# Attention and graph layers over 128 small graphs: the loop over the steps written out, and the instructions that carried its waits left out

## The chip, the cores and the metric

The kernel runs on one core of one Trainium2 chip. The metric is the device time of one execution in microseconds (us). TensorE (PE) has two clock levels, 1.2 and 2.4 GHz; a granted clock of 1.00 in the profile is the upper one.

## The reference

The input x holds 128 batches of 128 rows by 256 columns in float32, adj is one 128 by 128 matrix. Two layers are added to x one after the other:

```
h = relu(layernorm(x));            # over the 256 columns
A = adj @ h[b];  C = adj @ h[b] + bias
x = x + max over the columns of relu(A[:, None, :] + (C - A)[:, :, None])   # C - A = bias, so relu(max A + bias)
h = relu(layernorm(x))
q, k, v = split(h @ w_qkv);  8 heads of 32
a = softmax(where(adj == 0, -inf, q k^T / sqrt(32)));  o = (a v) @ w_proj + b_proj
x = x + o + layernorm(o) * gamma + beta
```

The first layer adds one number per row, so the second layernorm sees the same h as the first, and the kernel computes h once.

## The kernel before, in words

**Tiling.** A step handles four batches (G = 4), so there are 32 groups of work. Matrix products run in fp16 with a value split in a high and a low part, three products in place of one. The products with p_sb and v_sb, the softmax sums and the transposes are fp32.

**Stages.** A group passes through four consecutive steps t: products with adj and the projections to q, k, v (flag `a`), scores and their row maxima (`sc`, one step later), scores transposed, exponentials and their product with v (`e`, two later), normalising, projecting and storing (`d`, three later). So 32 groups take 35 steps, t = 0 to 34. In the middle every step has all stages at once, each of a different group.

**Order.** Each engine has its own instruction stream. In each, a list named `ORDER` names the pieces of a step, and `step(t, ...)` walks it. TensorE's list is
```
ORDER = ("K0 S0 S1 R0 S2 Q0 S3 R1 Q1 N0 E0 R2 O0 E1 E2 E3 L0 O1 R3 K1 S4 S5 O2 S6 S7 L1 O3 N1 M0 E4 E5 E6 "
         "P0 P1 Q2 P2 P3 Q3 P4 P5 E7 V0 P6 P7 V1").split()
```
K and N lay the mask into the four score banks of PSUM (`put_mask`, L339 to L346), S are scores (L368), M0 transposes the row maxima (L377), E transposed scores (L396), P the product with v and the sums (L416, L419), Q and V projections (L319, L332), L the first layer (L304), R and O the end of a group (L431, L443, L446). Engines wait for one another by counting semaphores: the k-th use waits for a value that grows with t.

**The loop.** `pipeline(eng, step)` runs steps 0 to 3 written out, then a loop in the hardware's sequencer (`eng.Fori`) over t = 4, 7, ..., 25 with three steps in its body (so 24 steps, 8 passes and 7 returns to its top), then steps 28 to 34 written out. Inside the loop the value of a wait is computed from the loop's register.

**Carriers.** Some instructions do no work of the kernel. In `put_mask` the first matmul (L339) writes one column that the next ones overwrite; it is there so that it takes the wait with a register's value. `act_cell` on ScalarE (L531), `dve_cell` on VectorE (L651, L713) and `carry_waits` on GpSimd (L822) are the same. They are in the written-out steps as well.

**Other places that are named below.** Row maxima: VectorE reduces each score bank (`row_max`, L674); M0 waits for all eight of them. The maxima then go through ScalarE (`max_high`, crow, L566) and VectorE (`max_low`, crow, L680), and P0 waits for that. The two fp16 parts of q and k go from `pairs` to `stack` by DMAs that SyncE (SP) issues: `stack_heads`, L273, twelve for each half of the heads, Q0 and Q1 of its list `C0 Q0 M0 Q1`; the scores S4 to S7 of the next step need those of Q1. ScalarE issues one transposing DMA a step (L532), ahead of its part of Q2. POOL is GpSimd.

Of the kernel before, what the change touches and what calls it, by code (L numbers as in the profile page):

```python
# [31 lines left out]
STEPS = B // G  # L32
P = 128
# [23 lines left out]
def build(nc, x, adj, bias0, w_qkv, w_proj, b_proj, gamma, beta, out):  # L57
# [3 lines left out]
    with ExitStack() as ctx:  # L61
# [38 lines left out]
        wp_hi = sb("wp_hi", [P, DC, D], F16)  # L100
        wp_lo = sb("wp_lo", [P, DC, D], F16)
        mhalf = sb("mhalf", [P, G])
        dve_cell = sb("dve_cell", [P, 2])
        pool_cell = sb("pool_cell", [P, 8])
        act_cell = sb("act_cell", [P, 1])

        x_sb = sb("x_sb", [P, SLOTS, G, D])
        y_sb = sb("y_sb", [P, G, D])
# [103 lines left out]

        def wait(eng, s, value):

            if not isinstance(value, int) or value > 0:
                eng.wait_ge(s, value)

        def pipeline(eng, step):


            def at(t):
                step(t, t % SLOTS, t < STEPS, 1 <= t <= STEPS, 2 <= t <= STEPS + 1, t >= 3, t + 1 < STEPS, t + 2 < STEPS,
                     t + 3 < STEPS)

            for t in range(SLOTS + 1):
                at(t)
            with eng.Fori(SLOTS + 1, STEPS - 2 * SLOTS, SLOTS) as t:
                for k in range(SLOTS):
                    step(t + k, (k + 1) % SLOTS, True, True, True, True, True, True, True)
            for t in range(STEPS - SLOTS - 1, STEPS + SLOTS):  # L230
                at(t)

        block = ctx.enter_context(nc.Block())

# [1 line left out]
        @block.sync  # L236
        def _(sp):
            nc.sync.dma_start(x_sb[:, 0], xg[0]).then_inc(x_loaded, 16)
            nc.sync.dma_start(adj_sb[:], adj).then_inc(core_load, 16)
            nc.sync.dma_start(w_sb[:], w_qkv.rearrange("(c p) n -> p c n", p=P)).then_inc(core_load, 16)  # L240
            nc.sync.dma_start(wp_sb[:], w_proj.rearrange("(c p) n -> p c n", p=P)).then_inc(c_load, 16)
            nc.sync.dma_start(bias0_sb[:], bias0.rearrange("(p o) -> p o", o=1)).then_inc(c_load, 16)
            for vec, dst in ((gamma, gamma_sb), (beta, beta_sb), (b_proj, bproj_sb)):
                nc.sync.dma_start(dst[:], vec.rearrange("(o d) -> o d", o=1).to_broadcast([P, D])).then_inc(c_load, 16)

            def copy_x(t):

                wait(sp, copied, 16 * t)
                nc.sync.dma_start(out.rearrange("(g b) n d -> g (b n) d", b=G)[t],
                                  x.rearrange("(g b) n d -> g (b n) d", b=G)[t]).then_inc(copied, 16)  # L250

            def max_rows(g, slot):

                for part, done in enumerate((chi_ready, clo_ready)):
                    sp.wait_ge(done, g + 1)
                    row = stack[STACK + part:STACK + part + 1, slot, 0].rearrange("p h b n -> p (h b) n")
                    nc.sync.dma_start(row, crow[:, part]).then_inc(crow_in, 16)

            def stack_heads(t, slot, j):
                if j == 0:  # L260

                    wait(sp, st_psum, UNITS * (t - 2))
                both = sp.snap(4 * t + 2 * j + 2) if not isinstance(t, int) else 4 * t + 2 * j + 2
                wait(sp, qkhi_ready, both)
                wait(sp, qklo_ready, both)
                for i in range(HC):
                    head = slice(HD * i, HD * (i + 1))

                    high = bass.AP(pairs[:].tensor, HD * i * PAIRS + 2 * j * G * N,
                                   [[PAIRS, HD], [(2 * DC + 1) * G * N, 2], [1, G * N]])  # L270
                    for blk, src in enumerate((high, pairs[head, 0, j], pairs[head, 1, j])):
                        dst = stack[blk * HD:(blk + 1) * HD, slot, :, HC * j + i]
                        nc.sync.dma_start(dst.rearrange("p s b n -> p s (b n)"), src).then_inc(stacked[j], 16)  # L273

            ORDER = ("C0 Q0 M0 Q1").split()

            def step(t, k, a, sc, e, d, prep, norm, load):
                for what in ORDER:
                    kind, i = what[0], int(what[1])
                    if kind == "C" and a:  # L280
                        copy_x(t)
                    elif kind == "Q" and a:
                        stack_heads(t, k, i)
                    elif kind == "M" and sc:
                        max_rows(t - 1, (k + 2) % SLOTS)

            pipeline(sp, step)


        @block.tensor  # L290
        def _(pe):
# [43 lines left out]
                mm.then_inc(v_psum, 1)  # L335

            def put_mask(mask):

                nc.tensor.matmul(sc_ps[0][:, 0, 0:1], identb[:], mask[:, 0, 0:1], start=True, stop=False,  # L339
                                 skip_group_check=True)  # L340
                for c in range(ROW_TILES):
                    for r in range(ROW_TILES):
                        rows = slice(HD * r, HD * (r + 1))
                        nc.tensor.matmul(sc_ps[r][HD * c:HD * (c + 1)], identb[rows, HD * r:HD * (r + 1)],  # L344
                                         mask[rows, c].unsqueeze(1).to_broadcast([HD, HC, N]), start=True, stop=False,
                                         skip_group_check=True)  # L346

            def mask_scores(g, j, e):

                if j == 0:  # L350
                    wait(pe, p_ready, UNITS * (g - 1))
                    if isinstance(g, int):
                        wait(pe, smax_ready, UNITS * g)
                elif e:
                    pe.wait_ge(p_ready, UNITS * (g - 1) + SC_SLOTS)
                else:
                    pe.wait_ge(smax_ready, UNITS * g + SC_SLOTS)
                put_mask(mask_q)
# [94 lines left out]
            O_BEFORE_M = sum(what[0] == "O" for what in ORDER[:ORDER.index("M0")])  # L453

            def step(t, k, a, sc, e, d, prep, norm, load):
                if isinstance(t, int) and t == 1:

                    pe.wait_ge(pool_const, 7)
                    pe.wait_ge(act_const, ACT_CONST)
# [30 lines left out]
                    elif kind == "O" and d:  # L490
                        project_o(t - 3, i, sc)

            pipeline(pe, step)


        @block.scalar
        def _(act):
            act.wait_ge(pool_zero, 4)
            act.wait_ge(adjT_ps, 1)
            nc.scalar.activation(adjT_hi[:], sc_ps[0][:, 0, :], ACT.Copy, scale=WS).then_inc(act_const, 1)  # L500
            act.wait_ge(core_load, 16 * 2)
# [24 lines left out]
            def transpose_h(t, par):  # L526
# [1 line left out]
                wait(act, v_psum, 2 * (t - 2))  # L528
                act.wait_ge(hhi_ready, G * (t + 1))
                act.wait_ge(hlo_ready, G * (t + 1))  # L530
                nc.scalar.activation(act_cell[:], pool_cell[:, 0:1], ACT.Copy)  # L531
                nc.scalar.dma_start_transpose(hT[:, par].rearrange("p a b c n -> p (a b c) n"),  # L532
                                              h_parts[:, par].rearrange("p a b d -> p (a b d)")).then_inc(hT_in, 16)

# [60 lines left out]
                     "E7 A2 V0 A3 V1 L0").split()  # L595

            def step(t, k, a, sc, e, d, prep, norm, load):
                if isinstance(t, int) and t == 1:
                    take_masks()
                for what in ORDER:  # L600
                    kind, i = what[0], int(what[1])
# [30 lines left out]
            load_x(2, 2)  # L632
            later_constants()
            transpose_h(0, 0)
            pipeline(act, step)


        @block.vector
        def _(dve):
# [8 lines left out]
            def aggregate_x(t):  # L648
                dve.wait_ge(stats1, G * (t + 1))
                wait(dve, norm1, 4 * t)  # L650
                nc.vector.memset(dve_cell[:, 0:1], 0.0)  # L651
                for b in range(G):
                    nc.vector.bn_aggr(mv1[:, b], st1[:, b]).then_inc(mv1_ready, 1)

# [54 lines left out]
            def aggregate_o(g):  # L709
                dve.wait_ge(stats2, G * (g + 1))  # L710
                wait(dve, norm2, 4 * g)
                wait(dve, tw_ready, G * g)
                nc.vector.memset(dve_cell[:, 1:2], 0.0)  # L713
                for b in range(G):
                    nc.vector.bn_aggr(mv2[:, b], st2[:, b]).then_inc(mv2_ready, 1)

# [88 lines left out]
            stats_x(1, 1)  # L805
            aggregate_x(1)
            later_constants()
            pipeline(dve, step)


        @block.gpsimd
        def _(pool):
# [4 lines left out]
                nc.gpsimd.affine_select(out=m[:], in_=m[:], compare_op=ALU.not_equal, fill=1.0, base=0,  # L817
                                        pattern=[[-1, P]], channel_multiplier=1).then_inc(pool_const, 1)

            def carry_waits(cell):  # L820

                nc.gpsimd.tensor_tensor(pool_cell[:, cell:cell + 1], pool_cell[:, 0:1], pool_cell[:, 0:1], ALU.add)  # L822

            def invert_std_x(t, par):

                pool.wait_ge(mv1_ready, G * (t + 1))
                wait(pool, h_ready, G * (t - 2))
                carry_waits(1)
                nc.gpsimd.tensor_scalar(ve1[:], mv1[:, :, 1], 1.0, EPS, ALU.mult, ALU.add).then_inc(norm1, 1)
                nc.gpsimd.tensor_scalar(negm1[:], mv1[:, :, 0], -1.0, 0.0, ALU.mult, ALU.add).then_inc(norm1, 1)  # L830
                pool.wait_ge(norm1, 4 * t + 1)
# [17 lines left out]
            def normalise_o(g):  # L849

                pool.wait_ge(mv2_ready, G * (g + 1))
                wait(pool, y_ready, G * g)
                carry_waits(3)
                nc.gpsimd.tensor_scalar(ve2[:], mv2[:, :, 1], 1.0, EPS, ALU.mult, ALU.add).then_inc(norm2, 1)
                nc.gpsimd.tensor_scalar(base2[:], mv2[:, :, 0], 1.0, 0.0, ALU.mult, ALU.add).then_inc(norm2, 1)
                pool.wait_ge(norm2, 4 * g + 1)
# [5 lines left out]
            def keep_l0(g, par):  # L862
                pool.wait_ge(l0_ready, g + 1)
                wait(pool, norm2, 4 * g)
                carry_waits(4)
                nc.gpsimd.tensor_scalar(l0_kept[:], l0[:, par], 1.0, 0.0, ALU.mult, ALU.add).then_inc(kept, 1)

            def widen(g, b):
                if b == 0:
                    pool.wait_ge(norm2, 4 * (g + 1))  # L870
                    carry_waits(2)
                nc.gpsimd.tensor_scalar(w2_sb[:, b], gamma_sb[:], rstd2[:, b:b + 1], 1.0,
                                        ALU.mult, ALU.add).then_inc(w2_ready, 1)

# [27 lines left out]
            def later_constants():  # L902
# [1 line left out]
                nc.gpsimd.memset(sel_sum[:], 0.0).then_inc(pool_zero, 1)  # L904
                nc.gpsimd.memset(sel_row[:], 0.0).then_inc(pool_zero, 1)
                nc.gpsimd.memset(lo_pick[:], 0.0).then_inc(pool_zero, 1)
                pool.wait_ge(pool_zero, 7)
                v = sel_sum[:].rearrange("p u (r e) -> p u r e", e=UNITS)
                nc.gpsimd.affine_select(out=v, in_=v, compare_op=ALU.not_equal, fill=SUM_SEL, base=0,
                                        pattern=[[1, UNITS], [0, HD // UNITS], [-1, UNITS]],  # L910
# [11 lines left out]
                    nc.gpsimd.memset(stack[STACK:ROWS, par, 1], MS).then_inc(ms_rows, 1)  # L922
                    pool.wait_ge(ms_rows, par + 1)

            nc.gpsimd.memset(pool_cell[:], 0.0).then_inc(pool_zero, 1)
            pool.wait_ge(pool_zero, 4)
            pool.wait_ge(dve_const, 1)
            invert_std_x(0, 0)
            for b in range(G):
# [1 line left out]
            later_constants()  # L931
            invert_std_x(1, 1)
            pool.wait_ge(c_load, 16 * 5)
            pipeline(pool, step)
            pool.wait_ge(stored, 16 * STEPS)


# [18 lines left out]
```

## Time and profile before

| | us |
|---|---|
| median of 3 runs | 870.18 (869.18 to 874.16) |
| the profiled execution | 871.38 |
| its span, from the first to the last instruction | 869.70 |
| PE busy | 765.6 (88%) |
| VectorE, ScalarE, GpSimd busy | 613.9, 500.7, 424.7 |
| mean granted clock | 0.957 |
| instructions in the trace | 31246, of them 22482 on PE (matmuls and weight loads) |

PE is the busiest engine. Its busy share is near full in all slices of the span but the first few and the last three. An idle time in a row stands in brackets with what ended it; "issue" there means that the engine waited for nothing that the profile shows. Matmuls of PE overlap, so the distance between two starts tells what one costs, not its own duration.

### The profile page before, as it was taken

What the parts mean: (1) busy time and instruction counts of PE and PEld (TensorE: products, weight loads), DVE (VectorE), ACT (ScalarE), POOL (GpSimd) and SP (SyncE); (2) the same over time, 40 slices, a digit from 0 to 9 for tenths busy, and PEclk for the clock granted to TensorE, in tenths of its full rate; (3) what the DMA queues carried; (4) which work ended last, traced back from release to release, by engine and by line L of the source; (5) the groups of instructions that cost most, each with busy time, mean ns of one, the idle gap of its engine ahead of it and who ended that gap; (6) DMA issues with size and microseconds to landing.
All of it is one profiled execution on the core that took longest, in us unless ns stands there. A gap on an engine that the chain in (4) does not pass through costs nothing.

```text
span 869.7 us, 31246 instructions
## 1 busy us (share of the span) xinstructions
PE 765.6 (88%) x11241; PEld 518.0 (60%) x11241; DVE 613.9 (71%) x1552; ACT 500.7 (58%) x1192; POOL 424.7 (49%) x853
## 2 busy tenths in 40 slices
PE   0668999989998998999899899899989999999662
PEld 0234666656665665666566566666666666666441
DVE  3744777767876775777688678677777777877642
ACT  3234665646665664566566566666656666665440
POOL 5712255554554454455545455545545555543442
PEclk9788999999999999999999999999999999999985
DMA  6265477865775767577587577677657777665331
GB/s 190 64 155 145 124 159 138 173 145 128 168 163 137 155 151 159 104 171 163 141 159 169 128 137 160 156 150 172 157 137 146 162 148 166 129 133 120 51 46 25
DMA packets 167271, 121.34 MB, mean 140 GB/s; under 512 B 83696, under 2 KB 166384, under 8 KB 166640
## 3 DMA queue, kind: packets, MB, share of 16 engines
q1 hardware_dynamic: 67328, 69.72, 30.6%
q10 hardware_dynamic: 82928, 33.04, 19.0%
q0 software_dynamic: 16896, 16.78, 14.2%
q8 instruction: 101, 1.65, 0.9%
q14 instruction: 18, 0.15, 0.1%
HBM read 35.06 MB, written 33.55 MB: 79 GB/s over the span
## 4 chain that ended last, share of the span: by engine, by line
PE 72%; issue 8%; ACT 6%; DVE 5%; SPq 3%; POOL 3%; DMA 2%; ACTq 1%; DVEq 0%; POOLq 0%
PE a_ps L319 17%; PE a_ps L332 9%; PE sum_ps L446 9%; PE pv_ps L416 8%; PE sc_ps L368 7%; PE sum_ps L419 6%; PE sc_ps L396 5%; PE sc_ps L344 4%; PE a_ps L304 4%; SPq L273 3%; DVE smax L674 2%; ACT h_sb L516 2%; PE pv_ps L431 2%; PE sum_ps L443 2%; ACT o_sb L590 1%
## 5 line engine op out<-in xcount | busy, mean ns | idle before, releaser
L674 DVE TENSOR_REDUCE smax<-sc_ps 128x4 f32<-128x512 f32 x256 | 164.8, 685 | 53.7 <-PE sc_ps L368 51.6
L571 ACT ACTIVATE p_sb<-sc_ps 128x512 f32<-128x512 f32 x256 | 145.8, 599 | 45.9 <-PE sum_ps L419 36.9
L666 DVE TENSOR_TENSOR pairs<-a_ps,pairs 128x512 f16<-128x512 f32 x128 | 87.5, 684 | 110.7 <-ACT pairs L561 110.2
L841 POOL TENSOR_TENSOR h_parts<-h_sb,h_parts 128x256 f16<-128x256 f32 x128 | 84.2, 669 | 141.5 <-ACT h_parts L524 141.2
L319 PE MATMUL a_ps<-hT,w_hi 128*128 128x512 f16 x512 | 141.0, 400 | 13.7 <-DMA hT<-h_parts 13.7
L847 POOL TENSOR_TENSOR oT_lo<-oT,oT_hi 128x256 f16<-128x256 f32 x128 | 85.6, 669 | 119.5 <-ACT oT_hi L584 119.3
L561 ACT ACTIVATE pairs<-a_ps 128x512 f16<-128x512 f32 x128 | 75.9, 594 | 97.8 <-PE a_ps L319 85.0
L416 PE MATMUL pv_ps<-p_sb,v_sb 128*32 128x128 f32 x2048 | 107.6, 279 | 20.1 <-DVE crow L680 10.3
L878 POOL DMA_DIRECT2D out<-y_sb x32 | 43.6, 1363 | 141.4 <-DVE y_sb L730 141.4
L419 PE MATMUL sum_ps<-p_sb,sel_sum 128*32 128x128 f32 x2048 | 105.3, 274 | 0.0
L368 PE MATMUL sc_ps<-stack 96*128 96x128 f16 x1024 | 86.0, 226 | 6.7 <-DMA stack<-pairs 6.5
L584 ACT ACTIVATE oT_hi<-oT 128x256 f16<-128x256 f32 x128 | 53.0, 414 | 66.7 <-DVE oT L703 66.7
L416 PEld LDWEIGHTS pv_ps<-p_sb,v_sb 128*32 128x32 f32 x2048 | 52.5, 109 | 58.6 <-issue 40.2
L368 PEld LDWEIGHTS sc_ps<-stack 96*128 96x128 f16 x1024 | 67.0, 101 | 31.0 <-issue 14.6
L319 PEld LDWEIGHTS a_ps<-hT,w_hi 128*128 128x128 f16 x512 | 44.6, 102 | 62.2 <-issue 16.6
L396 PE MATMUL sc_ps<-stack 98*128 98x128 f16 x1024 | 80.1, 222 | 0.0
L319 PE MATMUL a_ps<-hT,w_lo 128*128 128x512 f16 x256 | 79.1, 391 | 0.0
L332 PE MATMUL a_ps<-w_hi,hT 128*128 128x256 f16 x512 | 77.2, 273 | 1.5 <-DVE pairs L666 1.4
L516 ACT ACTIVATE h_sb<-x_sb,shift,rstd 128x256 f32<-128x256 f32 x128 | 72.1, 589 | 9.0 <-POOL shift L834 9.0
L396 PEld LDWEIGHTS sc_ps<-stack 98*128 98x128 f16 x1024 | 63.9, 99 | 15.1 <-issue 13.8
L590 ACT ACTIVATE o_sb<-sum_ps 128x256 f32<-128x256 f32 x128 | 48.7, 380 | 41.2 <-PE sum_ps L446 38.0
L703 DVE TENSOR_TENSOR oT<-pv_ps,pv_sb 128x256 f32<-128x256 f32 x128 | 53.3, 416 | 23.9 <-PE pv_ps L431 23.9
(103 smaller groups left out, 1504.2 us busy)
## 6 DMA issues: line engine op xcount, KB each, us to landing
stack<-pairs SPq DMA_DIRECT2D x768, 64.0 KB, 2.8
out<-in_x SPq DMA_DIRECT2D x32, 512.0 KB, 3.8
out<-y_sb POOLq DMA_DIRECT2D x32, 512.0 KB, 6.4
x_sb<-in_x ACTq DMA_DIRECT2D x31, 512.0 KB, 6.4
stack<-crow SPq DMA_DIRECT2D x64, 8.0 KB, 3.9
w_sb<-in_L_gnn_w_qkv SPq DMA_DIRECT2D x1, 768.0 KB, 6.0
x_sb<-in_x SPq DMA_DIRECT2D x1, 512.0 KB, 3.6
hT<-h_parts ACTq DMA_TRANSPOSE x32, 6.0
```

The costliest lines, as they stand in the source:

```text
L319: mm = nc.tensor.matmul(a_ps[c % 2][:].rearrange("p (b n) -> p b n", b=G), w[:, dc, col:col + P], hT[:, par, part, :, dc], start=(k == 0), ...
L332: mm = nc.tensor.matmul(a_ps[i][:, bb * D:(bb + 1) * D], hT[:, par, part, 2 * i + bb, dc], w[:, dc, 2 * D:3 * D], start=(k == 0), stop=(k ...
L368: mm = nc.tensor.matmul(to[:, i], stack[0:STACK, par, 0, h, b], stack[0:STACK, par, 1, h, b], start=False, stop=True, skip_group_check=True)
L396: mm = nc.tensor.matmul(to[:, i], stack[0:ROWS, par, 1, h, b], stack[0:ROWS, par, 0, h, b], start=False, stop=True, skip_group_check=True)
L416: nc.tensor.matmul(pv_ps[HD * i:HD * (i + 1), j], v_sb[:, par, b, HD * h:HD * (h + 1)], p_sb[:, u % P_SLOTS, i], start=True, stop=True)
L419: mm = nc.tensor.matmul(sum_ps[HD * i:HD * (i + 1), 0], sel_sum[:, u], p_sb[:, u % P_SLOTS, i], start=(u == 0), stop=(u == UNITS - 1), ski ...
L516: nc.scalar.activation(h_sb[:, b], x_sb[:, par, b], ACT.Relu, bias=shift1[:, par, b:b + 1], scale=rstd1[:, par, b:b + 1]).then_inc(h_ready, 1)
L571: nc.scalar.activation(p_sb[:, u % P_SLOTS], sc_ps[u % SC_SLOTS][:], ACT.Exp, scale=SCALE).then_inc(p_ready, 1)
L666: nc.vector.tensor_tensor(pairs[:, 1 - c % 2, c // 2, c % 2], a_ps[c % 2][:], pairs[:, c % 2, c // 2, c % 2], ALU.subtract).then_inc(qklo_ ...
L674: nc.vector.tensor_reduce(smax[:, HC * j:HC * (j + 1), b], sc_ps[u % SC_SLOTS][:], AX.X, ALU.max).then_inc(smax_ready, 1)
L841: nc.gpsimd.tensor_tensor(h_parts[:, par, 1, b], h_sb[:, b], h_parts[:, par, 0, b], ALU.subtract).then_inc(hlo_ready, 1)
L847: nc.gpsimd.tensor_tensor(oT_lo[:, b], oT[:, b], oT_hi[:, b], ALU.subtract).then_inc(olo_ready, 1)
```

## The change

The loop goes: all 35 steps are written out, so that each wait has a constant. The carriers go with their cells. A wait for the row maxima in `mask_scores`, which was made in the written-out steps alone, is now made in all. What is computed stays as it is.

```
-            if not isinstance(value, int) or value > 0:
+            if value > 0:
                 eng.wait_ge(s, value)
-        def pipeline(eng, step):
-            def at(t):
+        def pipeline(step):
+            for t in range(STEPS + SLOTS):
                 step(t, t % SLOTS, t < STEPS, 1 <= t <= STEPS, 2 <= t <= STEPS + 1, t >= 3, t + 1 < STEPS, t + 2 < STEPS,
                      t + 3 < STEPS)
-            for t in range(SLOTS + 1):
-                at(t)
-            with eng.Fori(SLOTS + 1, STEPS - 2 * SLOTS, SLOTS) as t:
-                for k in range(SLOTS):
-                    step(t + k, (k + 1) % SLOTS, True, True, True, True, True, True, True)
-            for t in range(STEPS - SLOTS - 1, STEPS + SLOTS):
-                at(t)
...
-                both = sp.snap(4 * t + 2 * j + 2) if not isinstance(t, int) else 4 * t + 2 * j + 2
-                wait(sp, qkhi_ready, both)
-                wait(sp, qklo_ready, both)
+                sp.wait_ge(qkhi_ready, 4 * t + 2 * j + 2)
+                sp.wait_ge(qklo_ready, 4 * t + 2 * j + 2)
...
             def put_mask(mask):
-                nc.tensor.matmul(sc_ps[0][:, 0, 0:1], identb[:], mask[:, 0, 0:1], start=True, stop=False,
-                                 skip_group_check=True)
...
-                    if isinstance(g, int):
-                        wait(pe, smax_ready, UNITS * g)
+                    wait(pe, smax_ready, UNITS * g)
...
-                nc.scalar.activation(act_cell[:], pool_cell[:, 0:1], ACT.Copy)
...
-                nc.vector.memset(dve_cell[:, 0:1], 0.0)
...
-                nc.vector.memset(dve_cell[:, 1:2], 0.0)
...
-            def carry_waits(cell):
-                nc.gpsimd.tensor_tensor(pool_cell[:, cell:cell + 1], pool_cell[:, 0:1], pool_cell[:, 0:1], ALU.add)
...
```

`carry_waits` was called once in each of `invert_std_x`, `normalise_o`, `keep_l0` and the first `widen` of a step.

## Rows read from the trace of the kernel before

**Rows 1.** The page, part 4: the chain that ended last, by engine.
```profile
PE 72%; issue 8%; ACT 6%; DVE 5%; SPq 3%; POOL 3%; DMA 2%; ACTq 1%; DVEq 0%; POOLq 0%
```

**Rows 2.** Busy time by stretch: stretch, us, PE, PEld, DVE, ACT, POOL, clock, DMA share, GB/s.
```profile
216.27:239.64 23.37, 22.94 (x354) 15.85 (x351) 18.52 (x49) 15.41 (x37) 12.53 (x27) 1.00 0.74 160
239.64:265.46 25.82, 23.09 (x353) 15.74 (x351) 19.03 (x50) 16.29 (x39) 15.22 (x31) 1.00 0.71 151
265.46:291.48 26.02, 24.73 (x351) 16.58 (x352) 17.81 (x46) 14.55 (x35) 9.94 (x23) 0.93 0.63 136
...
733.31:756.50 23.19, 22.94 (x354) 15.83 (x351) 18.65 (x49) 15.46 (x37) 12.48 (x27) 1.00 0.64 137
...
178.10:722.36 544.26, 515.94 (x7731) 353.13 (x7723) 408.04 (x1057) 339.04 (x815) 279.61 (x572) 0.98 0.70 151
```

**Rows 3.** PE in order of time around the loop's second return (start, us, what, [idle before]).
```profile
265.46 0.17 PE L339 MATMUL sc_ps<-mask_q,identb 128*128 128x1 bf16 x1 [2.30 <-issue]
...
266.89 1.91 PE L319 MATMUL a_ps<-hT,w_hi 128*128 128x512 f16 x4
```

**Rows 4.** Who waited for whom: us in total, times, longest.
```profile
PE sc_ps L339 <- issue: 15.2, 7, 2.5
...
PE pv_ps L416 <- ACT pv_sb L578: 9.8, 10, 1.6
```

**Rows 5.** PE in order of time, in a loop's step and in a written-out one.
```profile
253.19 0.43 PE L416 MATMUL pv_ps<-p_sb,v_sb 128*32 128x128 f32 x8 [0.38 <-DVE crow L680]
...
718.09 0.17 PE L339 MATMUL sc_ps<-mask_q,identb 128*128 128x1 bf16 x1
718.18 0.43 PE L344 MATMUL sc_ps<-mask_q,identb 32*32 32x512 bf16 x16
...
721.86 0.18 PE L339 MATMUL sc_ps<-mask_k,identb 128*128 128x1 bf16 x1
...
722.36 0.27 PE L377 MATMUL sum_ps<-identf,smax 128*32 128x128 f32 x1
...
723.50 0.43 PE L416 MATMUL pv_ps<-p_sb,v_sb 128*32 128x128 f32 x8 [0.19 <-DVE crow L680]
```

**Rows 6.** VectorE and ScalarE in order of time, same written-out step.
```profile
718.50 0.41 DVE L703 TENSOR_TENSOR oT<-pv_ps,pv_sb 128x256 f32<-128x256 f32 x1
718.99 0.69 DVE L674 TENSOR_REDUCE smax<-sc_ps 128x4 f32<-128x512 f32 x1
...
722.67 0.27 ACT L566 ACTIVATE crow<-sum_ps 32x128 f16<-32x128 f32 x1
```

**Rows 7.** ScalarE's queue and PE, and all 32 issues of L532 (ns min/median/max).
```profile
357.17 3.93 ACTq L532 DMA_TRANSPOSE hT<-h_parts  x1
...
362.19 0.43 PE L416 MATMUL pv_ps<-p_sb,v_sb 128*32 128x128 f32 x8 [1.47 <-ACT pv_sb L578]
...
L532 ACTq DMA_TRANSPOSE hT<-h_parts x32: 1440/1876/4029, 16.5 to 771.6; - x32
```

**Rows 8.** SP's queue, the chain, PE, and the landing of L273's DMAs.
```profile
753.01 9.53 SPq L273 DMA_DIRECT2D stack<-pairs  x12
...
761.95 3.41 DMA stack<-pairs
...
765.40 0.62 PE L368 MATMUL sc_ps<-stack 96*128 96x128 f16 x8 [0.41 <-DMA stack<-pairs]
...
DMA to landing us min/median/max: 2.0/2.8/6.6
```

**Rows 9.** GpSimd in order of time, in the last step.
```profile
857.56 0.19 POOL L822 TENSOR_TENSOR pool_cell<-pool_cell 128x1 f32<-128x1 f32 x1
857.74 2.18 POOL L872 TENSOR_SCALAR w_sb<-gamma_sb,rstd 128x256 f32<-128x256 f32 x4
```

**Rows 10.** The page, part 3: the queues that fetch instructions (packets, MB, share).
```profile
q8 instruction: 101, 1.65, 0.9%
q14 instruction: 18, 0.15, 0.1%
```

More of the change, by code:

```diff
@@ L102, in build @@
         mhalf = sb("mhalf", [P, G])
-        dve_cell = sb("dve_cell", [P, 2])
-        pool_cell = sb("pool_cell", [P, 8])
-        act_cell = sb("act_cell", [P, 1])
         x_sb = sb("x_sb", [P, SLOTS, G, D])
@@ L285, in step @@
                         max_rows(t - 1, (k + 2) % SLOTS)
-            pipeline(sp, step)
+            pipeline(step)
         @block.tensor
@@ L455, in step @@
             def step(t, k, a, sc, e, d, prep, norm, load):
-                if isinstance(t, int) and t == 1:
+                if t == 1:
                     pe.wait_ge(pool_const, 7)
@@ L491, in step @@
                         project_o(t - 3, i, sc)
-            pipeline(pe, step)
+            pipeline(step)
         @block.scalar
         def _(act):
-            act.wait_ge(pool_zero, 4)
             act.wait_ge(adjT_ps, 1)
@@ L597, in step @@
             def step(t, k, a, sc, e, d, prep, norm, load):
-                if isinstance(t, int) and t == 1:
+                if t == 1:
                     take_masks()
@@ L634, in _ @@
             transpose_h(0, 0)
-            pipeline(act, step)
+            pipeline(step)
         @block.vector
@@ L807, in _ @@
             later_constants()
-            pipeline(dve, step)
+            pipeline(step)
         @block.gpsimd
@@ L827, in invert_std_x @@
                 wait(pool, h_ready, G * (t - 2))
-                carry_waits(1)
                 nc.gpsimd.tensor_scalar(ve1[:], mv1[:, :, 1], 1.0, EPS, ALU.mult, ALU.add).then_inc(norm1, 1)
@@ L852, in normalise_o @@
                 wait(pool, y_ready, G * g)
-                carry_waits(3)
                 nc.gpsimd.tensor_scalar(ve2[:], mv2[:, :, 1], 1.0, EPS, ALU.mult, ALU.add).then_inc(norm2, 1)
@@ L864, in keep_l0 @@
                 wait(pool, norm2, 4 * g)
-                carry_waits(4)
                 nc.gpsimd.tensor_scalar(l0_kept[:], l0[:, par], 1.0, 0.0, ALU.mult, ALU.add).then_inc(kept, 1)
@@ L870, in widen @@
                     pool.wait_ge(norm2, 4 * (g + 1))
-                    carry_waits(2)
                 nc.gpsimd.tensor_scalar(w2_sb[:, b], gamma_sb[:], rstd2[:, b:b + 1], 1.0,
@@ L906, in later_constants @@
                 nc.gpsimd.memset(lo_pick[:], 0.0).then_inc(pool_zero, 1)
-                pool.wait_ge(pool_zero, 7)
+                pool.wait_ge(pool_zero, 6)
                 v = sel_sum[:].rearrange("p u (r e) -> p u r e", e=UNITS)
@@ L923, in later_constants @@
                     pool.wait_ge(ms_rows, par + 1)
-            nc.gpsimd.memset(pool_cell[:], 0.0).then_inc(pool_zero, 1)
-            pool.wait_ge(pool_zero, 4)
             pool.wait_ge(dve_const, 1)
@@ L933, in _ @@
             pool.wait_ge(c_load, 16 * 5)
-            pipeline(pool, step)
+            pipeline(step)
             pool.wait_ge(stored, 16 * STEPS)
```

## The prediction, on record before the changed kernel ran

> **What bounds the kernel now.** I read the chain that ended last first: TensorE (PE) holds 72% of it, and "issue", time that no wait explains, 8% [rows 1]. So I looked for what PE does that isn't work, and for where it stands still for nothing. Busy time by stretch, cut where a step of PE begins, gives three kinds of step [rows 2]: a plain step of the loop takes 23.37 us, the one before a return to the loop's top 25.82, the one after it 26.02, and the second of these has a granted clock of 0.93. A written-out step with all its work takes 23.19. PE in order of time shows both: the first instruction after the return stands behind 2.30 us of idle, and a little later four L319 matmuls take 1.91 us [rows 3]. The table of waits has this idle 7 times, 15.2 us in all [rows 4], once for each of the loop's 7 returns.
>
> From the row maxima's transpose of t = 6 to that of t = 28, which holds all seven returns, is 544.26 us [rows 2]. Twenty-two plain steps would be 22 x 23.37 = 514.1. So the returns and what follows them cost 30.1 us.
>
> In a plain step PE runs nearly without a gap (22.94 busy of 23.37), so what is taken from its stream comes off the time, as long as no other chain ends later. Two are near: VectorE and ScalarE around the row maxima, and SP's DMAs to `stack`. They decide how much of the small terms is kept.
>
> **The change part by part**, against the profiled execution: 871.38 us, of which the span is 869.70.
>
> *The returns.* The idle goes: 15.2 by the table, and about 1 more, because the last matmuls of the step still run out when the wait starts. What is left of 30.1 is 13.8. A part of that isn't the loop's. ScalarE's transposing DMA took 3.93 us to issue in one step, where the median is 1.88, and PE then waited 1.47 us for `pv_sb`, which ScalarE makes behind it [rows 7]. Between the two marks PE waited so three times (0.86, 1.47 and 1.20 us in its timeline; one of them is shown, and they are part of the 9.8 in [rows 4]), 3.5 us together. I leave that in: nothing in the change touches this DMA. The other 10 us goes with the lower clock that follows the idle (0.93 over a step [rows 2]). I take all of it as won, since no idle of that size is left in a middle step; the written-out ones have a clock of 1.00 [rows 2]. Term: 30.1 - 3.5 = **26.6**, with bounds of 16.2 (the clock falls all the same) and 30.1.
>
> Here the Trainium skill speaks, in sentences that the sum doesn't need. Its page "Advanced Engine Details and Errata", section "Control Flow Timing", gives about 108 ns for a compare-and-branch: seven returns would be an estimated 0.8 us, and the gain from the loop would nearly vanish. The rows show 2.30 us for one return [rows 3], so the trace doesn't agree. Its page "Runtime: NRT & Kernel Launch", section "Instruction fetch mechanics", says why a return may cost more: a taken branch to code that has left the small instruction memory waits for a fetch, while a stream in order is fetched ahead. The trace agrees with the first half on PE.
>
> *Waits with a register.* P0 waits for VectorE's crow; the idle is 0.38 us in a loop's step and 0.19 in a written-out one [rows 5]. That is the whole difference of 23.37 and 23.19. The register instructions on the other engines lie beside PE. Term: 24 x 0.18 = **4.3**; bounds 3 and 5.
>
> *The carriers on PE.* From the carrier to the next mask matmul is 0.09 to 0.10 us (718.09, 718.18) [rows 5]; there are four a step. Those of K0 and N0 lie in a stretch without gaps: 0.10 each. With K1's gone, S4 comes 0.10 earlier, and VectorE's reduction of it starts at 718.99, when VectorE has been free since 718.50 + 0.41 = 718.91 [rows 6], so 0.08 of it is kept. N1's stands behind the wait for the row maxima; without it M0 (722.36) comes 0.10 earlier, but ScalarE turns to crow at 722.67 straight from L516's work [rows 6], and has little room: 0.05. That is 0.33 a step, in the 29 steps from t = 3 to 31; in the first and last ones other waits take it up. Term: 29 x 0.33 = **9.6**; bounds 29 x 0.18 = 5.2 (the two after K1 give nothing and K0 gives 0.08) and 29 x 0.40 = 11.6.
>
> *The other carriers.* 857.56 to 857.74 is one of GpSimd's [rows 9]; with the gap ahead of it about 0.27. Two are in the closing chain, one in the opening one. Those of ScalarE and VectorE, and GpSimd's in the middle, hide behind PE. Term **1.0**, bounds 0.3 and 1.5.
>
> *The added wait for the row maxima in K0.* M0 of the step before has waited for the same value. 0.
>
> *What is given back.* Q3's values go to `stack` by 12 DMAs that SP issues in 9.53 us, and S4 of the next step needs the last one. In the written-out steps one S4 waited for it, 0.41 us [rows 8]: landing took 3.41 there. With the median of 2.8 it would have come 0.2 us before PE asked. So the chain ends within a fraction of a us of its use. The idle at each return let SP get ahead; that goes. And PE wants S4 0.3 us sooner. P0's earlier start helps the chain as much as PE, since it starts at Q3. If I take the scatter of one landing as it is, about one step in three waits 0.4 to 0.5 us: 0.15 a step, 28 steps, **-4.2**; bounds 0 and -9.
>
> Late transposing DMAs come in four middle steps of the 28 now, each a first step of the body. Whatever sets them, their place will no longer be fixed to the loop's top. I count 1.5 more at 1.3 us, **-2.0**; bounds +3.5 (none is left) and -9.
>
> The sum: 26.6 + 4.3 + 9.6 + 1.0 - 4.2 - 2.0 = 35.3; 871.38 - 35.3 = 836.1. The profiled execution is 1.2 us above the median of the runs shown (870.18), so on that scale **835** us. A full middle step should take 23.19 - 0.33 + 0.15 = 23.0.
>
> **The rivals.**
>
> *SP's chain sets the step.* For it: the wait at 765.40, and 9.5 us of issue that the change doesn't shorten. Against it: a single such wait in the written-out middle. If every step is held at 23.19, the 9.6 is lost and the 4.2 isn't paid: 836.1 + 9.6 - 4.2, so about 840 on the scale of the median. Chance 0.15.
>
> *More late transposing DMAs.* If it is one step in three, ten instead of four, at 1.3 us: 6 x 1.3 = 7.8, of which 2.0 is in the sum: 841. For it: 3.93 us occurs without a cause that the rows name. Against: none of the written-out steps from 28 on has one. Chance 0.12.
>
> *The clock falls all the same*, after the short waits that take the idle's place: 10 us, 845. Against it: plain steps with 0.38 us idle have 1.00 [rows 2, 5]. Chance 0.04.
>
> *Slower: the fetch of new code.* Two queues fetch code: one brought 1.65 MB, the other 0.15 [rows 10]. If the large one is PE's, that is 73 bytes for each of its 22482 instructions, and 17 for each of the 8764 of the others. So I take it that PE fetches the loop's body again in each pass, where nothing changes, and that the other engines keep theirs: 18 packets for 14 steps' worth of code (11 written out and the body's three). Writing out 21 steps more asks 18/14 x 21 = 27 more packets. If each stops an engine as the return stops PE, 2.30 us on the path, that is 62: 835 + 62 = 897. From 35/27 = 1.3 us each on the path it is slower than before. For it: a fetch that isn't ready costs 2.30 us on PE. Against: the steps from 28 on are such code for all engines, and hold 23.19. Chance 0.04.
>
> **How the numbers follow.** Forecast 0.65: 835, own range 829 to 840. The range for 8 in 10 runs from 828, where no DMA is late and the small terms are at their upper bounds, to 845, which takes in the three rivals that are still faster. Faster by over 0.5%: 0.95; within 0.5%, about what a measurement of this kernel tells from no change: 0.02; slower: 0.03. These two share the last rival's 0.04 and 0.01 more, for stops at fewer packets.
>
> **What would show it.** Right: no idle with "issue" ahead of K0's first mask matmul; clock 1.00 in every middle step; middle steps of 22.85 to 23.1 us; P0's idle 0.19 or somewhat more; S4 waiting for `stack` in some steps. Wrong in the carriers' term: steps that stay at 23.19. Wrong in what is given back: S4 waits in most steps or none, or PE waits for `pv_sb` behind issues of over 3 us in many. The sign is wrong if PE stands idle at new places for "issue", or waits for an engine that does.

## The result, and the profile after

The changed kernel takes **843.45 us** (median of 4 runs, 843.17 to 844.06) against 871.6 of the kernel before beside it (4 runs); the ratio is **0.968**, 95% interval 0.9645 to 0.971. Forecast was 835, with 829 to 840 as its own range and 828 to 845 as the wide one: the time lies outside the first and 1.55 us inside the second. The profiled execution took 843.20 us with a span of 841.3, so 28.2 us came off where the sum had 35.3. The chip has a slower state too: one run of the kernel before in the second group below and one of the kernel without K0's waits (its profiled one) were in it, so their times are left out and only distances between instructions are read from that profile.

From the page: the span, the chain of what ended last by engine (before: [rows 1]), and the queues that fetch code ([rows 10]).

```profile
span 841.3 us, 28575 instructions
PE 58%; DVE 13%; SPq 10%; issue 9%; DMA 4%; POOL 3%; ACT 3%; ACTq 1%; DVEq 0%; POOLq 0%
...
q10 hardware_dynamic: 82928, 33.04, 21.0%
q8 instruction: 89, 1.46, 0.7%
q14 instruction: 44, 0.36, 0.1%
```

PE's part of the chain fell from 72% to 58%, and SyncE's DMA issues rose from 3% to 10%: another chain now ends last in many steps. Other engines' code takes 26 packets more on q14, where the last rival had worked out 27; they did not cost 2.30 us each, since that would be 60 us.

Busy time by stretch (columns as in [rows 2]), cut at the transposes of the row maxima (M0): a clean step, a late one, and all from M0 of t = 6 to M0 of t = 28.

```profile
530.70:553.88 23.18, 22.86 (x348) 15.50 (x349) 18.57 (x47) 15.35 (x37) 11.73 (x22) 1.00 0.80 157
293.18:317.94 24.76, 23.04 (x347) 15.51 (x348) 18.51 (x47) 15.24 (x37) 11.74 (x22) 1.00 0.70 155
173.94:694.01 520.07, 504.79 (x7634) 341.05 (x7635) 407.48 (x1013) 336.21 (x793) 258.43 (x484) 1.00 0.76 159
```

The 22 steps took 544.26 before [rows 2] and 520.07 now. The clock is 1.00 throughout; before it was 0.98. But the clean step takes 23.18, as good as the 23.19 of the old written-out steps that had four PE carriers each. And 22 x 23.18 = 510.0, so 10.1 us lie in steps that are late.

Who waited for whom on PE (us in total, times, longest). The "issue" wait ahead of the mask, 15.2 us in [rows 4], is gone from the table.

```profile
PE sc_ps L352 <- DMA stack<-pairs: 10.9, 8, 4.3
PE pv_ps L400 <- ACT pv_sb L560: 9.8, 16, 1.1
PE pv_ps L400 <- DVE crow L661: 6.1, 30, 0.3
```

The same in the 22 steps alone, of the changed kernel and then of the one before, which had no wait for `stack` there:

```profile
PE pv_ps L400 <- ACT pv_sb L560: 5.0, 9, 0.8
...
PE sc_ps L352 <- DMA stack<-pairs: 2.8, 4, 1.2
```
```profile
PE pv_ps L416 <- ACT pv_sb L578: 3.5, 3, 1.5
```

The late step above, from the chain (start, us, what) and from PE in order of time. SyncE's twelve issues of Q1 have durations of 0.60 us, but one of 1.27, one of 2.28 and one of 1.46; the last lands 2.01 us later, and S4 has waited 0.65. PE had lost 0.74 in the same step before, behind a transposing DMA of 3.30 us.

```profile
303.72 1.27 SPq L261
...
306.96 2.28 SPq L261
...
310.57 1.46 SPq L261
312.03 0.04 issue
312.07 2.01 DMA stack<-pairs
314.08 0.05 issue
314.13 0.41 PE sc_ps L352 x4
```
```profile
299.96 0.42 PE L400 MATMUL pv_ps<-p_sb,v_sb 128*32 128x128 f32 x8 [0.74 <-ACT pv_sb L560]
...
314.13 0.62 PE L352 MATMUL sc_ps<-stack 96*128 96x128 f16 x8 [0.65 <-DMA stack<-pairs]
```

That chain also started late, at M0 + 8.55 in place of 7.46 of a clean step, because of ScalarE's transposing DMA. All its issues (ns min/median/max, to hold against [rows 7]), and one of them with what stands behind it:

```profile
L514 ACTq DMA_TRANSPOSE hT<-h_parts x32: 1431/2511/3746, 15.5 to 743.5; - x32
...
579.41 2.51 ACTq L514 DMA_TRANSPOSE hT<-h_parts  x1
...
582.02 0.60 ACT L543 ACTIVATE pairs<-a_ps 128x512 f16<-128x512 f32 x1 [2.20 <-issue]
...
580.91 2.37 SPq L246 DMA_DIRECT2D stack<-crow  x2
```

Its median rose from 1876 to 2511 ns. ScalarE's Q2 copy (582.02) stands behind it, then Q3's copy, then SyncE's twelve issues, then S4 of the next step. SyncE's two issues of crow (580.91, 2.37 together) run beside it and are long as well; the cause of all this is the last part of the next section.

### The profile page after: what moved, and what is told of

Same layout as the page of the kernel before. It is cut to its first block, busy times and chain, and to the rows that moved or that the text cites. A ratio compares the mean times of both kernels' runs of the same rounds, so it can differ in the third digit from the quotient of the medians.

```text
span 841.3 us, 28575 instructions
## 1 busy us (share of the span) xinstructions
PE 752.9 (89%) x11113; PEld 502.6 (60%) x11113; DVE 612.7 (73%) x1488; ACT 496.4 (59%) x1160; POOL 394.3 (47%) x724
## 3 DMA queue, kind: packets, MB, share of 16 engines
q10 hardware_dynamic: 82928, 33.04, 21.0%
q8 instruction: 89, 1.46, 0.7%
## 4 chain that ended last, share of the span: by engine, by line
PE 58%; DVE 13%; SPq 10%; issue 9%; DMA 4%; POOL 3%; ACT 3%; ACTq 1%; DVEq 0%; POOLq 0%
PE a_ps L307 13%; SPq L261 10%; DVE smax L655 9%; PE a_ps L320 7%; PE pv_ps L400 7%; PE sc_ps L380 6%; PE sum_ps L403 5%; PE sc_ps L329 5%; PE sum_ps L430 4%; PE sc_ps L352 4%; DMA stack<-pairs 3%; PE a_ps L292 2%; PE pv_ps L415 1%; POOL stack L894 1%; DVE st L688 1%
## 5 line engine op out<-in xcount | busy, mean ns | idle before, releaser
L655 DVE TENSOR_REDUCE smax<-sc_ps 128x4 f32<-128x512 f32 x256 | 164.4, 684 | 26.6 <-PE sc_ps L352 24.7
L307 PE MATMUL a_ps<-hT,w_hi 128*128 128x512 f16 x512 | 135.6, 388 | 13.8 <-DMA hT<-h_parts 13.8
L352 PE MATMUL sc_ps<-stack 96*128 96x128 f16 x1024 | 84.3, 222 | 11.0 <-DMA stack<-pairs 10.9
L352 PEld LDWEIGHTS sc_ps<-stack 96*128 96x128 f16 x1024 | 65.3, 99 | 34.3 <-DMA stack<-pairs 14.7
L320 PE MATMUL a_ps<-w_hi,hT 128*128 128x256 f16 x512 | 77.2, 273 | 1.9 <-DVE pairs L647 1.9
L380 PEld LDWEIGHTS sc_ps<-stack 98*128 98x128 f16 x1024 | 63.8, 99 | 15.1 <-issue 13.8
```

Of the source, the lines that this page charges most:

```text
L307: mm = nc.tensor.matmul(a_ps[c % 2][:].rearrange("p (b n) -> p b n", b=G), w[:, dc, col:col + P], hT[:, par, part, :, dc], start=(k == 0), ...
L320: mm = nc.tensor.matmul(a_ps[i][:, bb * D:(bb + 1) * D], hT[:, par, part, 2 * i + bb, dc], w[:, dc, 2 * D:3 * D], start=(k == 0), stop=(k ...
L352: mm = nc.tensor.matmul(to[:, i], stack[0:STACK, par, 0, h, b], stack[0:STACK, par, 1, h, b], start=False, stop=True, skip_group_check=True)
L380: mm = nc.tensor.matmul(to[:, i], stack[0:ROWS, par, 1, h, b], stack[0:ROWS, par, 0, h, b], start=False, stop=True, skip_group_check=True)
L655: nc.vector.tensor_reduce(smax[:, HC * j:HC * (j + 1), b], sc_ps[u % SC_SLOTS][:], AX.X, ALU.max).then_inc(smax_ready, 1)
```

## The experiments

Twelve kernels in three groups; each group shares runs of the kernel before (medians 872.0, 872.86 and 871.75 us of 11, 10 and 11 runs). Single runs of one kernel spread over up to 12 us, so I read medians of six (five without K0's waits), and profiled steps beside them. The letters of the theories come from the expectations, which stand as they were recorded.

### Does the gain need more than TensorE's stream?

**Only TensorE written out**, the others keep loops, all keep carriers.
```
-            pipeline(pe, step)
+            pipeline(pe, step, True)      # for t in range(STEPS + SLOTS): at(t)
```


> The kernel before with only TensorE's steps written out; the four other engines keep their loops and all engines keep their carriers. Theory A with the whole gain coming from TensorE's own returns and register waits: 842 to 845 us, about as the changed kernel. Since the other engines then fetch little code (queue q14 about 18 packets as before instead of 44), the theory that code packets lengthen the transposing DMA's issue expects fewer issues over 3.0 us than the changed kernel's 7 in the middle, and a time up to 5 us lower: 839 to 843. Theory F: carriers 9.6 and 1.0 still paid, 852 to 855 us.

849.69 us, ratio 0.9737 (0.9694 to 0.978): between the two forecasts. PE has no idle at returns any more, though four engines still take theirs; the returns' cost was PE's alone. The clean step is 23.37, and P0's idle stays as in a loop's step [rows 5], although every wait of PE is now a constant (the last row is M0 of t = 6 to M0 of t = 28, as in all fences like it below):

```profile
554.68 0.43 PE L420 MATMUL pv_ps<-p_sb,v_sb 128*32 128x128 f32 x8 [0.38 <-DVE crow L684]
...
176.46:696.35 519.89, 505.63 (x7731) 348.50 (x7723) 408.63 (x1057) 338.69 (x815) 280.86 (x572) 1.00 0.76 158
```

So the 0.18 a step belonged to the loops of the engines that PE waits for; that it is their register waits is the likely reading, not a separate test. With q14 back at 18 packets the time isn't lower, so 26 packets more of code aren't what the changed kernel pays for. This kernel has 5.8 us in late steps (519.89 - 22 x 23.37), the changed one 10.1.

**A loop of six steps**, 3 returns for 7.
```
-            with eng.Fori(SLOTS + 1, STEPS - 2 * SLOTS, SLOTS) as t:
-                for k in range(SLOTS):
+            with eng.Fori(SLOTS + 1, STEPS - 3 * SLOTS, 2 * SLOTS) as t:
+                for k in range(2 * SLOTS):
```


> The kernel before with a loop body of six steps in place of three, so 3 returns in place of 7, and all register waits and carriers kept. If each return costs its share of the 30.1 us that the trace of before put on them (3.8 us net each): 15 us under the kernel before, 856 to 858 us. Rival (the gain of writing out comes mostly from the register waits, which stay): 868 us or more.

860.75 us, ratio 0.9884 (0.9844 to 0.9923). The idle goes with the returns (first row; 15.2 us in 7 in [rows 4], so 2.8 each in place of 2.2), and the time by 12.1 us for four of them, 3.0 each. That is under the 3.8 expected: the idle that is left is longer, and three steps without a return near them (t = 25, 27, 28) are now late by 0.4 to 0.7 us. I take it that a return's idle also let SyncE catch up; no run shows it by itself.

```profile
PE sc_ps L339 <- issue: 8.4, 3, 2.9
...
178.10:710.99 532.89, 509.83 (x7732) 349.75 (x7723) 409.03 (x1057) 338.81 (x815) 279.31 (x572) 0.99 0.73 155
```

### What were the carriers worth?

**TensorE's carrier back in the changed kernel.**
```
+                nc.tensor.matmul(sc_ps[0][:, 0, 0:1], identb[:], mask[:, 0, 0:1], start=True, stop=False, ...)
```


> The changed kernel with TensorE's carrier alone put back at the head of each mask block (4 in a full step). Theory A: no change, 843 to 844.5 us; the carrier's matmul shows between the full matmul and the first mask matmul, which stay 0.20 us apart. Theory F: 0.33 us in each of 29 steps, 853 us.

**Every carrier kept, all steps written out.**
```
 for t in range(STEPS + SLOTS): at(t)      # in the kernel before, no Fori
```


> All 35 steps are written out on every engine, but every carrier instruction of the kernel before is kept. Theory A (TensorE's carriers lay in a gap of 0.20 us that the small weight load of the mask's first matmul leaves behind a full matmul anyway): the same time as the changed kernel, 843 to 845 us, and the cleanest middle step still 23.18 us. Theory F (the prediction's: the carriers stood in TensorE's own chain, 0.33 us per step): 843.45 + 9.6 + 1.0 = 854 us, cleanest middle step 23.5 us.

The clean step is 23.19 in both, so theory F falls. Beside V1's last matmuls, PE in order of time and its weight loads, of the changed kernel and then of the one with the carrier back:

```profile
564.61 0.38 PE L320 MATMUL a_ps<-w_lo,hT 128*128 128x256 f16 x2
564.92 0.43 PE L329 MATMUL sc_ps<-mask_q,identb 32*32 32x512 bf16 x16
...
564.92 0.14 PEld L329 LDWEIGHTS sc_ps<-mask_q,identb 32*32 32x32 bf16 x16 [0.21 <-issue]
```
```profile
588.12 0.38 PE L320 MATMUL a_ps<-w_lo,hT 128*128 128x256 f16 x2
588.34 0.17 PE L326 MATMUL sc_ps<-mask_q,identb 128*128 128x1 bf16 x1
588.44 0.43 PE L331 MATMUL sc_ps<-mask_q,identb 32*32 32x512 bf16 x16
```

From L320's pair to the first mask matmul is 0.31 us without a carrier and 0.32 with one. Without it the mask's weight load has 0.21 us of idle ahead of it; with it the carrier stands there.

**Is that gap the wait's?** The changed kernel without K0's waits in the middle.
```
-                    wait(pe, p_ready, UNITS * (g - 1))
-                    wait(pe, smax_ready, UNITS * g)
+                    if g == 0 or g > STEPS - 2:
+                        ...
```


> The changed kernel without the two waits ahead of the first mask block of each middle step, which are already fulfilled by what TensorE waited for earlier. Theory A (the gap of 0.20 us ahead of the mask's first weight load comes from the small weight load behind a full matmul): gap unchanged at 0.15 to 0.20 us, time within 1 us of the changed kernel's 843.45. Theory B (the gap comes from the wait that the first weight load carries): the gap closes at that block, some 0.1 us in each of 27 steps, 840.5 to 841 us.

```profile
592.60 0.38 PE L320 MATMUL a_ps<-w_lo,hT 128*128 128x256 f16 x2
592.91 0.43 PE L329 MATMUL sc_ps<-mask_q,identb 32*32 32x512 bf16 x16
...
592.91 0.14 PEld L329 LDWEIGHTS sc_ps<-mask_q,identb 32*32 32x32 bf16 x16 [0.21 <-issue]
```

The same 0.31 and 0.21 with no wait there at all: theory B falls. (846.15 us, ratio 0.9699, 0.9651 to 0.9747.) The gap stands where the weight load goes from 128 rows to 32, and a carrier in it costs nothing. The type of the operands changes there too, from float16 to bfloat16, and no run tells the two apart.

The whole times say less. Theory A expected about 843 to 845 of all three. With all carriers it is 841.68 us (0.9651, 0.961 to 0.9691), a little *under* the changed kernel; with TensorE's alone 848.51 (0.9739, 0.9703 to 0.9775), 5 over, which the clean step doesn't explain. The first trace has something new: its transposing DMA takes 1.9 us again, and Q1 starts at M0 + 7.46 in nearly every step. So I went after that.

### What made the transposing DMA's issue longer?

**The changed kernel again, as a control.**


> The changed kernel once more, unaltered, as the control for the others of this group. 843 to 846 us; transposing DMA's issue 2.5 us in the median, some seven of 22 middle steps lengthened by S4's wait for the stack.

**One engine's carriers back at a time.** ScalarE's stands right ahead of the DMA:
```
+                nc.scalar.activation(act_cell[:], pool_cell[:, 0:1], ACT.Copy)
                 nc.scalar.dma_start_transpose(...)
```


> The changed kernel with ScalarE's carrier alone put back: one copy of a 128x1 cell right ahead of the transposing DMA. Theory C (that carrier kept the DMA's issue short: 1.93 us with it, 2.54 us without): the issue is back at 1.9 to 2.0 us in the median with none over 3.0, Q1's stack chain starts at M0 + 7.46 in nearly every step, and the time is some 5 us under the control's, 838 to 841 us. Rival (the short issue comes from the carriers of GpSimd or of VectorE, or from anything else in the kernel that keeps all carriers): issue stays at 2.5 us, time within 1 us of the control.

GpSimd's and VectorE's, with their cells behind all other buffers:
```
+                carry_waits(1)                             # GpSimd, 4 a step
+                nc.vector.memset(dve_cell[:, 0:1], 0.0)    # VectorE, 2 a step (the other kernel)
```


> The changed kernel with GpSimd's four carriers per step put back, their cell allocated after all other SBUF buffers so that no buffer moves. Theory G (GpSimd's carriers kept the transposing DMA's issue short): issue 1.9 us in the median, Q1's chain starts at M0 + 7.46 in nearly every step, 840 to 842 us. Theories V (VectorE's carriers did) and M (the place of the buffers in memory did): issue stays at 2.4 to 2.5 us, 844 to 849 us.

> The changed kernel with VectorE's two carriers per step put back, their cell allocated after all other buffers. Theory V: issue 1.9 us, 840 to 842 us. Theories G and M: issue stays at 2.4 to 2.5 us, 844 to 849 us.

**No carrier, but the buffers where they were.**
```
         mhalf = sb("mhalf", [P, G])
+        dve_cell = sb("dve_cell", [P, 2])
+        pool_cell = sb("pool_cell", [P, 8])
+        act_cell = sb("act_cell", [P, 1])
         x_sb = sb("x_sb", [P, SLOTS, G, D])
```


> The changed kernel with no carrier back, but the three unused cells allocated where the kernel before had them, so that every buffer behind them lies at its address of before. Theory M (the addresses decide how long the transposing DMA's issue takes): issue 1.9 us, 840 to 842 us. Theories G and V: issue 2.4 to 2.5 us, 844 to 849 us.

| kernel | cells at their old place | issue, median ns | PE's waits for `stack` and for `pv_sb`, us, all steps | M0(6) to M0(28) | over 22 clean steps of 23.18 (23.19 with PE's carriers) | median us | ratio (95%) |
|---|---|---|---|---|---|---|---|
| changed | none | 2511 | 10.9, 9.8 | 520.07 | 10.1 | 843.45 | 0.968 (0.9645 to 0.971) |
| control | none | 2360 | 16.7, 7.9 | 521.29 | 11.3 | 844.55 | 0.9686 (0.964 to 0.9731) |
| PE's back | none | 2432 | 12.5, 9.7 | 520.23 | 10.1 | 848.51 | 0.9739 (0.9703 to 0.9775) |
| ScalarE's back | two of three | 2400 | 18.0, 10.6 | 525.05 | 15.1 | 848.96 | 0.9741 (0.97 to 0.9782) |
| GpSimd's back | at the end | 2418 | 16.8, 8.3 | 524.13 | 14.2 | 847.70 | 0.9714 (0.9669 to 0.9759) |
| VectorE's back | at the end | 2281 | 16.1, 7.4 | 522.54 | 12.6 | 847.91 | 0.9744 (0.9696 to 0.9792) |
| **no carrier** | **all three** | **1922** | 12.8, 4.7 | **513.94** | **4.0** | **837.89** | 0.9627 (0.9581 to 0.9673) |
| all carriers | all three | 1922 | 12.8, 4.7 | 515.31 | 5.1 | 841.68 | 0.9651 (0.961 to 0.9691) |

The two kernels with all three cells in place have 1922 ns and at most 5.1 us in late steps; all others have 2281 and more, and 10 to 15 us. Which carriers run makes no difference to it. The other six profiles fall on the same two sides: 1876 ns before, 1868 and 1980 in the two kernels with loops and 1848 in the last one below, all with the cells in place; 2504 without K0's waits and 2450 in the last but one, without all of them. With ScalarE's carrier back two cells are in place, 36 of the 44 bytes, and that doesn't do it. The last step from none to all cells changes not one instruction; it moves the buffers behind them by 44 bytes a partition as declared. **Theory M holds**, C, G and V fall. The same instructions in its trace (to hold against the rows at 579.41, 582.02 and 580.91 above), and its 22 steps:

```profile
571.98 1.94 ACTq L517 DMA_TRANSPOSE hT<-h_parts  x1
...
574.02 0.60 ACT L546 ACTIVATE pairs<-a_ps 128x512 f16<-128x512 f32 x1 [1.63 <-PE a_ps L310]
...
572.99 1.68 SPq L249 DMA_DIRECT2D stack<-crow  x2
...
q10 hardware_dynamic: 82928, 33.04, 19.3%
...
172.19:686.13 513.94, 503.39 (x7634) 341.08 (x7635) 408.61 (x1013) 337.74 (x793) 258.95 (x484) 1.00 0.77 160
```

ScalarE's copy now waits for PE's matmul and no longer for the issue. Queue q10, which holds the transposing DMA, moves the same 82928 packets in less time, 19.3% in place of 21.0% of the 16 engines' span. By its median it is 6.7 us under the control. The two intervals overlap (0.964 and 0.9673) and the kernels ran in different groups, so the times alone would not settle it; the split of the profiles by one property does, for the issue and for the 22 steps. What it is worth in whole time is less sure than that it is there.

The four kernels with one engine's carriers back came out 3 to 4 us over the control, and the one without K0's waits 1.6 us. Three of the four lose more in late steps than the control's 11.3, PE's does not, and nothing that I ran tells why.

### The chain made shorter

Since SyncE's twelve issues end last in many late steps, the last two of Q1 go to ScalarE, after its last work of the step; first with ScalarE's carrier (buffers moved), then with all carriers.
```
+                        if j == 1 and i == HC - 1 and blk > 0:
+                            continue                       # SyncE
...
+                for blk in (1, 2):                         # ScalarE, after L0
+                    nc.scalar.dma_start(stack[...], pairs[head, blk - 1, 1]).then_inc(stacked[1], 16)
```


> The kernel with ScalarE's carrier back, and the last two of Q1's twelve stack DMAs issued by ScalarE after its last instruction of the step instead of by SyncE. If SyncE's chain of twelve issues sets S4 in the steps over 23.2 us: it ends 1.3 us earlier, S4 waits in few steps, middle steps 23.2 us, 4 to 6 us under the kernel with the carrier back (834 to 837 us). Rival (ScalarE's issues delay its own copies at the head of the step, or slow SyncE's that run beside them): no gain, or 1 to 10 us slower than that kernel.

> The written-out kernel with every carrier kept, and the last two of Q1's twelve stack DMAs issued by ScalarE at the end of its step. The kernel with all carriers had 15 of 22 clean middle steps and lost 5.1 us in the others, all of it to S4's wait; the moved issues take that away: 835 to 837 us, 2 to 3 us under the 838.4 us of the same move with ScalarE's carrier alone. If the short transposing issue of the kernel with all carriers does not matter once the chain is shorter: the same 838 to 839 us.

838.43 us (0.9622, 0.9584 to 0.966) and **834.77 us** (0.9575, 0.9535 to 0.9615; single runs 833.96 to 837.15), both under the changed kernel. The first is 10.5 us under the same kernel without the move, where 4 to 6 were expected. PE's waits for `stack` without and with the move, and the second one's 22 steps:

```profile
PE sc_ps L363 <- DMA stack<-pairs: 12.8, 8, 4.5
```
```profile
PE sc_ps L365 <- DMA stack<-pairs: 1.4, 5, 0.3
...
172.16:685.98 513.82, 505.82 (x7731) 348.55 (x7723) 410.57 (x1057) 339.38 (x815) 278.08 (x572) 1.00 0.77 160
```

The first fence is the kernel with all carriers, the second the same with the DMAs moved. S4 hardly waits any more. But the 22 steps gained only 1.5 us over the kernel with all carriers (515.31); the rest came ahead of them, where M0 of t = 6 moved from 178.12 to 172.16, since the two longest waits for `stack` (4.5 and 3.0 us) were in the first steps. So the time was as expected and the place only in part.

## Why the prediction was right, and where it was wrong

**The returns: right.** 26.6 was forecast for them. No "issue" wait is left ahead of the mask, the clock is 1.00, and TensorE's stream alone does it: with that alone written out the lateness of the 22 steps fell from 30.1 to 5.8 us. The idle ahead of K0 was the price, with its lower clock; the rival in which the clock falls all the same is out.

**Waits with a register: right in size.** 23.37 became 23.18, P0's idle 0.19. The sum had charged it to waits with a register and let those of the other engines lie beside PE; they don't: what costs it sits on the engines ahead of P0, not on PE.

**The carriers on PE: wrong, 9.6 forecast, nothing found in the middle.** The prediction put a price on the distance from the carrier to the next matmul (718.09 to 718.18, [rows 5]) and took it that this distance would close. It doesn't: the next instruction, a load of 32 by 32 weights, leads to a mask matmul 0.31 us after L320's pair without a carrier and 0.32 with one. [rows 5] told what follows the carrier, not what stands there without it. That is 22 x 0.33 = 7.3 us in the 22 steps, most of the 8.4 us between 835 and 843.45. The sign that the prediction had set for it, steps that stay at 23.19, came. In its rival "SP's chain sets the step" the steps stay there too, at about 840, but for a reason that didn't hold: a clean step has no wait for `stack`.

In the first steps the carriers may count: M0 of t = 6 came at 178.1 before and with all of them kept, at 172.2 to 174.9 without any, and the kernel with all of them is 3.8 us over the one with none and the same addresses (two groups of runs). But with all carriers and the two DMAs moved it came at 172.16. One part can be named: PE's first matmul on `h_parts` starts at 33.1 to 34.6 us in the seven profiles with ScalarE's carrier and at 31.7 to 31.8 in the seven without. In those seven kernels ScalarE also waits at its start for the memset of the carrier's cell, and no run parts the two. The rest is open.

**What is given back: the right size by luck, two errors that cancel.** In the 22 steps the sum left 3.5 us for late transposing DMAs, and gave back 22 x 0.15 = 3.3 for S4's waits and 2.0 for more late ones: 8.8 in all. Measured were 10.1. But "nothing in the change touches this DMA" was false. The change took out three small cells, and that moved its buffers: 6.1 of the 10.1 go when they move back. The waits of the 22 steps with the old addresses, no carrier:

```profile
PE pv_ps L403 <- DVE crow L664: 4.4, 22, 0.3
PE sc_ps L355 <- DMA stack<-pairs: 3.3, 5, 1.0
```

Of the 4.0 us of lateness 3.3 are S4's waits for `stack`, in 5 of the 22 steps, where the kernel before had none (with all carriers 4.4, also in 5): this term was forecast right, at 3.3. And PE no longer waits for `pv_sb` at all, so the 3.5 us that the sum left in would have gone with the returns (the last section has the issues behind them). So of the 8.8 the 3.3 were right, the other 5.5 would not have come, and 6.1 that no term had came with the buffers in their place. The rival "more late transposing DMAs" named what came, at a price (841) 2.5 us under the result, with no mechanism.

**The added wait: 0, right.** **Fetch of new code: right that it doesn't cost.** 26 packets more came, and the kernel without them was no faster: it loses 5.8 us in late steps with 18 packets on q14, and the kernel with all carriers 5.1 with 45, at the same addresses.

**The sum again**, over the 22 steps: 30.1 (returns and lateness of before) + 22 x 0.19 (the waits) - 10.1 (lateness now) = 24.2, which is 544.26 - 520.07; the terms are read from the two profiles, so the sum has to come out. Another 4.2 came before M0 of t = 6, and nothing behind M0 of t = 28. The time lies in the wide range, near its end, because the largest term, the returns, was right; with the 7.3 us of the carriers taken out the sum says 842.3.

## What to carry to other kernels

A loop's return is worth removing on the engine that bounds the kernel; elsewhere it lies beside other work, and only its register waits show. Before you price an instruction that only carries a wait, find out what would stand in its place: on TensorE the gap ahead of the 32-row weight load held it for free here. And a change that removes or adds a buffer moves all buffers behind it; hold the addresses still in one experiment, or its effect is credited to the instructions.

## What the runs showed that I had not expected

- The addresses of SBUF buffers changed how long a transposing DMA takes to issue: 1922 ns in the median against 2360 and 2511, with the same instructions and the same 82928 packets. Which buffer matters, and what property of its address, I did not try.
- Code packets may lengthen single issues. In the kernel with no carrier and the old addresses the four longest of the middle steps (2.51, 2.44, 2.41 and 2.35 us) each had a packet of q8 start between 0.2 us ahead of the issue and 0.4 behind its start. None reached 3.0; in the changed kernel, with as many packets, seven did. Against a fixed rule: with all carriers kept four middle issues had such a packet, and took 2.60, but also 1.93, 2.07 and 2.09.
- The late transposing DMAs of the kernel before, whose place the prediction could not explain, go with PE's loop. Its four issues over 3 us behind the first one (4.03, 3.32, 3.93 and 3.66) stand behind M0 of t = 4, 10, 13 and 22, all first steps of the body, and in each a packet of q8 starts 1.3 to 2.5 us after the issue's start. The loop of six steps has four such as well (3.58, 3.16, 3.20 and 3.88), at t = 4, 10, 16 and 22: its entry and its three returns, with the packet 1.4 to 1.6 us in. q8 is PE's: writing out PE alone took it from 101 packets to 90 and left q14 at 18. PE waits 3.5 us for `pv_sb` in the 22 steps of either. In the four kernels with PE written out and the old addresses no issue behind the first is over 2.76 us, and PE waits 0 to 0.6 us for it. The three at the returns of the loop of six steps:

```profile
279.12 3.16 ACTq L532 DMA_TRANSPOSE hT<-h_parts  x1
...
425.46 3.20 ACTq L532 DMA_TRANSPOSE hT<-h_parts  x1
...
570.00 3.88 ACTq L532 DMA_TRANSPOSE hT<-h_parts  x1
```

- TensorE's step stayed at 23.18 to 23.19 with 0, 1 or all carriers, and the 32-row mask load began 0.20 us after the start of the last full matmul in the median of its places behind L320's pair, and 0.31 and 0.15 behind the other two kinds of matmul that run ahead of a mask block without a pause.
